# Perceiver block on one core: values made for all eight heads at once, and a longer lag behind them

## The reference, cut to what matters

```
n = layernorm(x)
q = (n @ Wq), k = (context @ Wk), v = (context @ Wv)      # 8 heads of 64
x = x + softmax(q k^T / 8) v @ Wo + bo
x = x + attention over the 128 tokens (softmax over the query axis), weights aq, ak, av
x = x + feed-forward, hidden width 2048, float-quantised hidden values and weights
```

## Time and profile before

| | us |
|---|---|
| median of 3 runs | 923.07 (923.06 to 923.19) |
| the profiled execution, own time | 923.73 |
| its span in the trace | 921.7 |
| TensorE busy | 905.2 (98%) |
| weight loads, VectorE, ScalarE, GpSimd busy | 565.6, 548.3, 576.5, 507.4 |
| chain that ended last: TensorE's share | 94% (values 28%, keys 27%) |
| waits of GpSimd for p_f, of VectorE for k_h and v | 233.4, 126.3, 112.5 |

### The profile page before, as it was taken

The page is one execution under the profiler, slowest core; times in us unless marked ns, Lnnn a source line. Parts: engine busy times, 40 slices in busy tenths (PEclk is TensorE's granted clock), DMA queues, the critical chain, the costliest instruction groups (busy, mean ns, idle before and its releaser), DMA issues.

```text
span 921.7 us, 19492 instructions
## 1 busy us (share of the span) xinstructions
PE 905.2 (98%) x7470; PEld 565.6 (61%) x7470; DVE 548.3 (59%) x973; ACT 576.5 (63%) x1014; POOL 507.4 (55%) x393
## 2 busy tenths in 40 slices
PE   7999999999999999999999999999999899999998
PEld 4556666666666666666666666666666455544444
DVE  6645565555555555655555565556667669886633
ACT  4756777776677777777776677777567423236540
POOL 4636567556555755675576556778876755310000
PEclk9999999999999999999999999999999999999999
DMA  9377576676657566565666666857997462223502
GB/s 339 84 150 161 138 132 136 159 142 144 144 132 139 127 144 142 128 143 140 139 153 144 143 138 141 198 132 149 182 189 157 92 127 70 71 85 74 183 12 81
DMA packets 340267, 126.35 MB, mean 137 GB/s; under 512 B 316112, under 2 KB 317904, under 8 KB 340176
## 3 DMA queue, kind: packets, MB, share of 16 engines
q1 hardware_dynamic: 324832, 95.87, 49.4%
q10 hardware_dynamic: 15344, 29.23, 10.6%
HBM read 45.36 MB, written 2.10 MB: 51 GB/s over the span
## 4 chain that ended last, share of the span: by engine, by line
PE 94%; ACT 2%; DVE 1%; DMA 1%; issue 1%; SPq 1%; ACTq 0%; DVEq 0%
PE v_ps L670 28%; PE k_ps L670 27%; PE e_ps L739 10%; PE e_ps L670 8%; PE o_ps L759 6%; PE o_ps L761 3%; PE e_ps L1021 3%; PE o_ps L776 2%; PE o_ps L1014 1%; PE e_ps L1014 1%; PE o_ps L954 1%; PE v_ps L1014 1%; SPq L636 1%; DMA raw<-in_ctx_t 1%; PE k_ps L1014 0%
## 5 line engine op out<-in xcount | busy, mean ns | idle before, releaser
L1979 POOL TENSOR_TENSOR p_l<-p_f,p_h 128x1024 f16<-128x1024 f32 x128 | 273.1, 2134 | 233.4 <-ACT p_f L1202 233.4
L1537 DVE TENSOR_REDUCE q_max<-e_ps 128x1 f32<-128x1024 f32 x128 | 153.4, 1219 | 48.9 <-PE e_ps L739 48.9
L1530 DVE TENSOR_TENSOR k_l<-k_ps,k_h 128x512 f16<-128x512 f32 x128 | 88.5, 691 | 126.3 <-ACT k_h L1166 126.3
L1523 DVE TENSOR_TENSOR v<-v_ps,v 128x512 f16<-128x512 f32 x127 | 87.8, 691 | 112.5 <-ACT v L1158 112.5
L1195 ACT ACTIVATE p_h<-e_ps,bias 128x1024 f16<-128x1024 f32 x128 | 143.3, 1120 | 2.4 <-issue 0.3
L1202 ACT ACTIVATE p_f<-e_ps,bias 128x1024 f32<-128x1024 f32 x128 | 142.1, 1111 | 0.0
L670 PE MATMUL v_ps<-wv_h,ctx_h 128*128 128x256 f16 x756 | 124.4, 273 | 1.7 <-DVE v L1523 1.7
L670 PE MATMUL v_ps<-wv_l,ctx_h 128*128 128x256 f16 x756 | 123.7, 273 | 0.0
L670 PE MATMUL v_ps<-wv_h,ctx_l 128*128 128x256 f16 x756 | 123.7, 273 | 0.0
L759 PE MATMUL o_ps<-v,pt_h 128*128 128x128 f16 x1024 | 104.2, 220 | 0.7 <-DVE acc L1554 0.7
L670 PE MATMUL k_ps<-ctx_h,wk_h 128*128 128x512 f16 x384 | 103.8, 379 | 0.0
(11 more groups left out here) (311 smaller groups left out, 1286.9 us busy)
## 6 DMA issues: line engine op xcount, KB each, us to landing
raw<-in_ctx_t ACTq DMA_DIRECT2D x27, 768.0 KB, 5.5
w_raw<-in_w_t SPq DMA_DIRECT2D x32, 256.0 KB, 4.0
raw<-in_ctx_t SPq DMA_DIRECT2D x4, 768.0 KB, 7.5
pt_h<-p_h SPq DMA_TRANSPOSE x128, 2.8
pt_l<-p_l SPq DMA_TRANSPOSE x128, 2.8
out<-xr SPq DMA_DIRECT2D x7, 256.0 KB, 2.0
x_in<-in_x SPq DMA_DIRECT2D x6, 256.0 KB, 8.4
o_all<-in_x ACTq DMA_DIRECT2D x6, 256.0 KB, 3.7
```

The lines of the kernel that those rows point to most:

```text
L1523: dve.tensor_tensor(v[g][:, j0:j0 + 2, :, DH:VW], v_bank(s)[:, :].rearrange("p (j h d) -> p j h d", j=2, d=DH), v[g][:, j0:j0 + 2, :, 0:DH ...
L1530: dve.tensor_tensor(k_l[:, s // 2 % K_RING, cols], k_ps[:, :], k_h[:, s // 2 % K_RING, cols], ALU.subtract)\
L1537: ins = dve.tensor_reduce(q_max[:, col:col + 1], e_ps[s % 2][:, :, :].rearrange("p i n -> p (i n)"), AX, ALU.max, negate=True)
L1979: pool.tensor_tensor(p_l[:, s % L_RING, :, :], p_f[:, s % F_RING, :, :], p_h[:, s % H_RING, :, :], ALU.subtract).then_inc(p_split, 1)
```

## The change

Slots 0 to 7 stay as they were. From slot 8 on `value_tiles` makes one tile of context for all eight heads: 9 matmuls of 512 columns. The two value tensors become one, so that a copy can write all heads of a tile. The values of a half are therefore all needed and all made half by half, and the context's halves are kept for two halves and not for two batches (the two copies of a half in steps 8n+1 and 8n+2), with three raw buffers. Exponentials, scores and weighted values lag two slots more. The weighted values use one bank, the other is joined with the key bank for later use. The first stage's key weights lie in five pieces and one aside, so that the memory holds the next stage's projection weight beside the context. The tables of extras are new, VectorE sums weighted values after `v_low` and `k_low`, and the tail after the slots is interleaved anew. Cut to its core:

```diff
-K_RING = 4
+K_RING = 3
+HALVES = SLOTS // PER_HALF
+RAW_RING = 3
...
-        o_ps = [psum("o_ps0", [P, 512]), psum("o_ps1", [P, 512])]
+        o_ps0 = psum("o_ps0", [P, 512])
+        k_ps, s_ps = m_ps[:, 0, :], m_ps[:, 1, :]
+        o_ps = [o_ps0, s_ps]
...
-        X_LAG, PV_LAG = 3, 5
+        X_LAG, PV_LAG = 5, 7
+        WEIGHT_LOADS = {113: (0, 1), 114: (2, 3), 116: (4,), 117: (5,), 118: (6,), 119: (7,), 120: (8,), 121: (9,), 122: (10,),
+                        123: (11,), 124: (12,), 125: (13,), 126: (14, 15)}
+        WEIGHT_HIGH = {115: (0, 1), 117: (2, 3), 119: (4, 5), 121: (6, 7), 123: (8, 9), 124: (10, 11), 126: (12,), 127: (13,), 128: (14, 15)}
+        WEIGHT_LOW = {116: (0,), 117: (1,), 118: (2,), 119: (3,), 120: (4,), 121: (5,), 122: (6,), 123: (7,), 124: (8,),
+                      125: (9, 10), 126: (11,), 127: (12,), 129: (13, 14, 15)}
...
-            return s // PER_BATCH, s % PER_HALF // 4, s % PER_BATCH // PER_HALF * PER_HALF + 2 * (s % 4)
+            return (s // 4, 2 * (s % 4), 2) if s < PER_HALF else (None, s % PER_BATCH, 1)
...
-        WEIGHT_BEHIND = {111: 0, 112: 1, 114: 2, 115: 3, 117: 4, 118: 5, 120: 6, 121: 7}
-        LOAD_X = {100: 6, 101: 7, 102: 0, 103: 1, 104: 2, 105: 3, 106: 4, 107: 5}
-        ADD_BIAS = {104: (6, 7, 0), 106: (1,), 108: (2, 3, 4), 110: (5,)}
+        WEIGHT_BEHIND = {115: (0,), 117: (1, 2), 118: (3,), 119: (4, 5), 120: (6,), 121: (7,)}
+        LOAD_X = {104: 0, 105: 1, 106: 2, 107: 3, 108: 4, 109: 5, 110: 6, 111: 7}
+        ADD_BIAS = {111: (0,), 114: (1, 2), 116: (3,), 118: (4, 5), 120: (6,), 122: (7,)}
...
-        for n in range(1, STAGES):
-            if QUARTERS + n < B * QUARTERS:
-                ctx_behind[QUARTERS * n + 2] = QUARTERS + n
...
+        for hb in range(1, HALVES):
+            at = PER_HALF * hb
+            ctx_behind[at - 7], ctx_behind[at - 6] = 2 * hb, 2 * hb + 1
+            if hb > 1:
+                load_behind[at - 12], load_behind[at - 9] = 2 * hb, 2 * hb + 1
...
-                cols = wv_cols(g)
-                for j in (j0, j0 + 1):
...
+                cols, wide = (slice(0, D), D) if g is None else (wv_cols(g), D // 2)
+                for j in range(j0, j0 + n):
...
-                if s >= 2:
-                    pe.wait_ge(acc_ready, s - 1)
+                if s:
+                    pe.wait_ge(acc_ready, s)
...
-                if s % 2 == 0 and 2 <= s < SLOTS:
-                    scores(s // 2 - 1)
+                if s % 2 == 0 and s >= 4:
+                    scores(s // 2 - 2)
...
-                if 0 <= s - SLOTS + 19 < 2 * CC:
-                    load_weight(s - SLOTS + 19)
-                if 2 * CC <= s - SLOTS + 20 < 16:
-                    load_weight(s - SLOTS + 20)
+                for i in WEIGHT_LOADS.get(s, ()):
+                    load_weight(i)
```

TensorE after the slots:

```diff
-            weighted_values(SLOTS - PV_LAG)
+            weighted_values(SLOTS - 7)
+            scores(UNITS - 2)
+            fold(0)
+            weighted_values(SLOTS - 6)
+            project_out(0)
+            weighted_values(SLOTS - 5)
+            project_out(1)
             scores(UNITS - 1)
-            fold(0)
-            project_out(0)
-            for r in range(1, 4):
-                weighted_values(SLOTS - PV_LAG + r)
-                project_out(r)
+            weighted_values(SLOTS - 4)
+            fold(1)
+            weighted_values(SLOTS - 3)
+            project_out(2)
+            project_out(3)
+            weighted_values(SLOTS - 2)
             project_out(4)
-            fold(1)
+            project_out(5)
             weighted_values(SLOTS - 1)
-            project_out(5)
             project_out(6)
             bias_products()
             fold(2)
```

More of the change, by code:

```diff
@@ L167, in perceiver_kernel @@
      p_sum, o_den, shift) = keep.values()
+    bv_row, a21 = rows["bv_row"], list(odd_keys.values())
     q_h, q_l = queries.values()
@@ L1214, in _ @@
             k_high(0)
-            wk_high(slice(P, D))
+            for n in range(1, 4):
+                wk_high(n)
             ctx_high(1)
@@ L2055, in _ @@
                     p_low(s - X_LAG)
-                if s >= FIRST_SPLIT and s % 2 == 0:
-                    weight_high(s - FIRST_SPLIT)
-                    weight_high(s - FIRST_SPLIT + 1)
+                for i in WEIGHT_HIGH.get(s, ()):
+                    weight_high(i)
                 done = s - PV_LAG - 1
@@ L2075, in add_norm @@
                 pool.tensor_tensor(xr[:, r, :], xr[:, r, :], o_all[:, r, :], ALU.add).then_inc(x1n_ready, 1)
+            p_low(SLOTS - 5)
+            for i in WEIGHT_HIGH[SLOTS]:
+                weight_high(i)
+            o_norm(STAGES - 4)
+            p_low(SLOTS - 4)
             p_low(SLOTS - 3)
+            o_norm(STAGES - 3)
             p_low(SLOTS - 2)
-            o_norm(STAGES - 3)
+            inverse_deviation(0)
             p_low(SLOTS - 1)
+            o_norm(STAGES - 2)
+            inverse_deviation(1)
             def norm_low(what, r):
```

340 lines of the change are left out of this document (183 added, 157 removed).

## The result

The changed kernel takes 952.86 us (952.64 to 957.1, 4 runs), the kernel before, on the same chip, 923.13 (923.06 to 923.42, 4 runs). The ratio, over all these executions, is 1.033, with a 95% interval of 1.0304 to 1.0361: slower by some 3%. The profiled execution took 952.78, its span 950.7, at a mean granted clock of 0.989 (before: 923.73, 921.7, 0.997).

What follows compares the result with a forecast made beforehand. TensorE, 98% busy, was taken as the bound. -3.6 - 0.5 + 1.8 + 13.0 + 6.8 + 7.0 = +24.5 on 923.73 gives 948.2 profiled, 947 for the median; own range 941 to 953, overall 931 to 956.

Steps and rivals of the forecast that it cites:

- values: 120 of 128 slots: 9 matmuls of 512 columns for 18 of 256, saving 0.03 us a slot: -3.6 us.
- lag, start: Kernel start: 1.5 us early wait goes, first pair's second exponential late by 0.7; net -0.5 (-1.5 to +1).
- context copies: Copy after an odd step pushes the second exponential: 0.3 us in six pairs with a fade, +1.8 (0 to +4).
- loads of the last weights: Steps 113 and 114: loads waiting in ScalarE's queue delay TensorE, +6.4 and +4.9, plus +1.7 slow clock: +13.0 us.
- end of the slots: Steps 115 to 121: late GpSimd and SyncE's queue of transposes make TensorE wait; 11.9 against 5.1 now, +6.8 (0 to +9).
- folded tail: After the slots: waits of 1.7 (slot 125's sum) and 3.8 (last projection), 1.5 for the clock: +7.0 us (0 to +10).
- The first wait: Step 113: exponential stands behind loads 0 and 1, which wait for ctx_low(30); scores at 15.6 for 9.2, +6.4 us.
- The second: Step 114: load 3 waits for ctx_low(31); value subtraction ends at 26.5, TensorE done at 21.7: +4.9 us.
- A: ScalarE stalls at the loads, but SyncE and GpSimd keep up and the tail is as good as now: 933.8, chance 0.22.
- B: Loads cost nothing because ctx_low(30) ends before 8.0 us into the pair, and the end's waits are filled: 915.7, chance 0.1.
- C: Waits feed on each other: late value copies drop the clock again, p_h and p_l rings fill; about 957, chance 0.13.
- The signs: Changed profile: ScalarE idle 5 us twice near 640, TensorE waits on p_f, value subtraction, pt_l, q_h/q_l; values at 216 ns.

Runs made afterwards that it cites:

- experiment 5: The changed kernel with the two copies of a context half in even steps 8n+2 and 8n+4, not 8n+1 and 8n+2: 951.67 us.
- Experiment 3: The changed kernel with each tile of values made as two halves of 256 columns, 18 matmuls for 9, into the same bank: 960.26 us.
- Experiment 11: The changed kernel with ScalarE issuing loads 0, 1 and 2 in step 114 and load 3 in step 115, not in 113 and 114: 946.1 us.
- Experiment 6: On top of experiment 1, high halves of weights 0 to 7 made by ScalarE in steps 116 to 122, not by GpSimd: 939.72 us.
- experiment 1: The changed kernel with loads 0 to 3 of the last weights issued by SyncE, four steps sooner, not by ScalarE: 946.2 us.
- experiments 8, 9 and 10: Experiment 6 plus later output and norm turning, then cumulatively: one weight turned per slot, 935.18 us; mends at traced waits, 936.4; w1_high back and aq rehomed, 931.1.
- Experiment 4: The changed kernel with GpSimd making the last heads' output ahead of norm 2's low half, and SyncE turning them in that order: 953.65 us.

## Why the prediction was right, and where it was off

The forecast, 947 in a range of its own of 941 to 953, holds the measured 952.86, just: one of the four executions, 957.1, lies outside it. The mechanism is the one forecast, in place and order; the size is off by 6. Some of the agreement is luck: the loads were forecast 1.9 too dear and the end of the slots 5.2 too cheap. Profiled, +29.05 against +24.5. Term by term:

| term | forecast | measured |
|---|---|---|
| values | -3.6 | -2.7 |
| lag, start | -0.5 | -1.2 |
| context copies | +1.8 | +2.2 |
| loads of the last weights | +13.0 | +11.1 |
| end of the slots | +6.8 | +12.0 |
| folded tail | +7.0 | +7.0 |
| sum | +24.5 | +28.4 |

The 0.6 us between this sum and the profiled +29.05 have a place too. Behind a wait TensorE's next matmul stood some 0.15 us further from the one ahead of it than the row's idle time and the usual distance make. The four pairs of 11.21, 12.14, 11.07 and 16.31 us up to 724.16 hold 0.62 more than their rows and 1.7 of clock; the later ones at 730.07, 734.81 and 743.73 hold another 0.5. Against that, the changed kernel is 0.66 shorter behind the folded tail (161.84 us from the first `e_ps<-at_h,f_h` to the end, for 162.50), where a wait of 0.46 for `tt_l` is gone.

**Values.** 9 matmuls fewer give 0.023 us a slot (experiment 5 against before), 2.7 in 120. The 0.03 came from differences of rows rounded to 0.01 us. Experiment 3 gives the same 0.023 once its two long issues are left out. The matmuls of 512 columns run at 0.216 in the changed kernel too. The Trainium skill ("TensorE: Matmul & The Clock Gate", Wait — 56ns, not 53.3ns?) puts the fixed part of one matmul at about 2.5 ns beside its columns; as an estimate from that figure nine of them make 0.0225 us. The measured 0.023 agrees. The Trainium skill (same page, Back-to-back issue gap) has 131 ns for a stream of weight loads and 512-column matmuls; the 216 ns of every run here do not agree.

**The start.** Step 113 begins at 631.78, 4.17 us sooner than before (635.95). 2.76 of this is work put off by the longer lag, two slots of weighted values and a pair of scores. The other 1.4 is 2.4 of values (106 slots) less 2.2 of copies, and so 1.2 of the start. Of this, 0.35 is no effect of the change: the first context came at 6.31 us, for 6.66 before, and between 6.37 and 6.99 in the experiments. The early wait went, as forecast; a wait of 0.56 for `p_f` at 64.41 is new, where 0.7 had been counted for the first pair.

**Copies.** Six waits of 0.25, where 0.3 was forecast. The pairs that hold them are 0.32 longer than the others, 1.9 in all, and two pairs behind them are 0.07 and 0.18 longer, for which no row was found; both go in experiment 5.

**Loads.** The first wait is right: 6.27 for 6.4. (The prediction's 2.9 from the exponential to its read should be 2.8 by its own rows; 2.84 was measured.) The second ends where it was forecast, 26.35 us into the pair (658.13 - 631.78) for 26.5. What was wrong is the clock on top. I had let TensorE run at full speed to that point and be done at 21.7; at half clock it needed 2.9 more, and was done 1.91 before the values came. So 2.9 of clock and 1.91 of wait, 4.8, are together the 4.9 forecast, and the 1.7 charged beside it was in it already. Together 11.1 for 13.0. Experiment 11 shows the cause directly: one step later, and the first block doesn't occur.

**The end of the slots** is the step that failed. Measured are waits of 0.41, 1.34, 0.28, 3.83, 2.38 and 3.90, 12.1 together; 3.3 of clock (18 matmuls in 5.57 us for 3.88 behind 717.82, 1.6 more behind 734.81); and 1.65 at 743.73, where `project_out(0)` waited for VectorE to finish low halves of the last pieces: 17.1, less the 5.1 of before. Forecast were 1.3, 3.9, 4.6, 0.6 and 1.5 of clock, 11.9. Two figures were too small. The first is when pt_l(115) can be turned: from the start of step 119 (674.83) p_low(115) ended after 16.8 us, at 691.62, and not after 14.8. At least in part this is GpSimd's two high halves, which take 3.1 to 3.6 and not 3.0. The second is the price of an issue, 1.44 on average and not 1.34, 2.8 us over 28. By both, the wait for pt_l(121) had to end 4.8 later than the 55.1 forecast, and it ended 4.9 later (734.81, 60.0 into the pair). Besides, the 1.65 on VectorE was left out altogether. GpSimd's two waits for turned weights, 3.61 and 2.75, were not seen coming either, but they cost the queue nothing: it has no gap while they last. Experiment 6 tries the first figure: with eight high halves off GpSimd, pt_l(115) is turned 10.2 us sooner than in experiment 1 and the kernel wins 6.5. That the issues behind it must all pass, however they are spread, agrees with experiments 8, 9 and 10.

**The tail.** 1.64, 3.80 and 1.56 for 1.7, 3.8 and 1.5. Experiment 4 shows that GpSimd's norm_low(2) ahead of o_norm(31) makes the second.

**The rivals.** A (933.8: SyncE and GpSimd keep up) needed TensorE's stall to be their gain. TensorE did stall 8.2 us there, and from pt_l(115) on the queue was full all the same. B (915.7: the loads cost nothing) fell on its own condition: ctx_low(30) had to end 8.0 us into the pair and ended at 643.57, 11.8 into it. C (957, the waits feed on each other) is met in its number by the slowest execution, 957.1, of which there is no trace. In the trace of the change its mechanism is not seen: behind the late values of 658.13 the clock stayed at 1.00.

**The signs** that were named came: ScalarE idle 5.91 and 6.08 us, released by `ctx_l`; TensorE waiting for `p_f` and for the subtraction; values at 0.216; waits for `pt_l` near slot 120; `q_l` before the last projection.

## What to carry to other kernels

A DMA issue that waits for a semaphore holds up everything behind it on its engine (here ScalarE, 5.91 and 6.08 us): when steps are shifted, ask of every load what its wait will find at the new place, and move the load by a step before anything else. When the same number of transposes is to go through one queue in fewer slots, first hold their count times a measured mean per issue, not the shortest one, against that time, and ask when the first of them can start, which may be another engine's doing; spreading them differently inside the full stretch only renames the waits. Waits that one full queue makes may not be added up as gains of separate mends. And where a wait's end is set by another engine, a slow clock ahead of it is part of the wait and not a price beside it (here 2.9 of clock and 1.91 of wait make up the 4.9 forecast).
